# Eight-head attention on one Trainium2 core: the softmax is divided before the transposes on ScalarE instead of after the value product on VectorE, with a new order on every engine

## What is computed

```python
x = L0(x, ...)   # batch norm, 3x3 depthwise conv, 4-head attention on 7x7 keys, conv, 1x1, MLP
x = L1(x, ...)   # group norm, linear attention (softmax of k and of q apart), projection
# L2, the third layer
hid = group_norm(x, 32 groups)                      # (b, 256, 196)
q, k, v = split(einsum('oc,bcl->bol', qkv_w, hid) + qkv_b)      # 8 heads of 32 channels
weight = softmax(einsum('bhct,bhcs->bhts', q * scale, k * scale), axis=-1)
a = einsum('bhts,bhcs->bhct', weight, v)
x = x + einsum('oc,bcl->bol', proj_w, a) + proj_b
x = L3(x, ...)   # group norm, 1-head attention over 196 positions, projection, residual
```

## Time and profile before

| what | value |
|---|---|
| time, median of 3 runs | 2169.7 us (2168.6 to 2170.22) |
| the profiled execution's own time | 2170.37 us |
| its span, first to last instruction | 2168.3 us |
| mean granted TensorE clock | 0.976 |
| busy: PE, PEld | 2076.3 us (96%), 1686.7 us (78%) |
| busy: DVE, ACT, POOL | 1820.4 us (84%), 1527.8 us (70%), 1278.3 us (59%) |

### The profile page before, as it was taken

One profiled execution on the slowest core, in us unless ns is written; L12 is line 12 of the kernel. 1 busy time (PEld: TensorE's weight loads), 2 busy tenths in 40 slices (PEclk: granted clock), 3 DMA queues, 4 the chain that ended last, 5 costly groups with the idle time before them and its releaser, 6 DMA issues.

```text
span 2168.3 us, 58678 instructions
## 1 busy us (share of the span) xinstructions
PE 2076.3 (96%) x15232; PEld 1686.7 (78%) x15232; DVE 1820.4 (84%) x4359; ACT 1527.8 (70%) x5172; POOL 1278.3 (59%) x2954
## 2 busy tenths in 40 slices
PE   4679999999999999999999999999999999999987
PEld 3466888888888788888878888887888888788775
DVE  6778899988888998988899898888989888887532
ACT  2256777777777777777777777777777777777763
POOL 2455666666666666666666666666666666664311
PEclk8799999999999999999999999999999999999977
DMA  3000011001101100110110011011101100100000
GB/s 126 15 23 23 16 39 39 29 23 37 37 22 37 37 30 22 37 37 22 37 37 30 22 37 37 23 36 37 37 15 37 37 31 28 38 31 24 24 23 23
DMA packets 29828, 70.22 MB, mean 32 GB/s; under 512 B 6261, under 2 KB 7105, under 8 KB 29761
## 3 DMA queue, kind: packets, MB, share of 16 engines
q1 hardware_dynamic: 26928, 67.68, 9.0%
q10 hardware_dynamic: 2832, 1.73, 0.3%
HBM read 30.86 MB, written 12.85 MB: 20 GB/s over the span
## 4 chain that ended last, share of the span: by engine, by line
PE 91%; DVE 3%; POOL 2%; issue 2%; ACT 1%; SPq 1%; DMA 0%; POOLq 0%; DVEq 0%; ACTq 0%
PE ps_c L1166 19%; PE ps_a L1166 17%; PE ps_e L1166 17%; PE ps_b L1166 17%; PE ps_s L1166 10%; PE ps_s L1216 8%; POOL gn_t L579 1%; PE ps_a L1292 1%; DVE y L1158 1%; PE ps_e L1454 0%; PE ps_e L1292 0%; PE ps_b L1454 0%; PE ps_e L1399 0%; SPq L475 0%; ACT e L827 0%
## 5 line engine op out<-in xcount | busy, mean ns | idle before, releaser
L827 ACT ACTIVATE e<-ps_s,nm 98x196 f32<-98x196 f32 x1024 | 426.1, 446 | 89.9 <-DVE nm L956 89.8
L590 POOL TENSOR_SCALAR xn<-x,gn_scale,gn_shift 128x196 f32<-128x196 f32 x384 | 353.2, 933 | 20.8 <-POOL gn_shift L585 20.8
L1158 DVE SCALAR_TENSOR_TENSOR y<-opad,w_dw,y 128x406 f32<-128x406 f32 x512 | 301.8, 645 | 0.0
L1139 DVE SCALAR_TENSOR_TENSOR y<-xpad,w_dw,y 128x406 f32<-128x406 f32 x512 | 300.8, 640 | 0.0
L956 DVE TENSOR_REDUCE nm<-ps_s 98x4 f32<-98x784 f32 x256 | 240.6, 962 | 41.8 <-PE ps_s L1166 41.8
L834 ACT COPY pt<-ps_s 98x392 f32<-98x392 f32 x512 | 229.1, 503 | 42.6 <-PE ps_s L1216 41.8
L568 POOL TENSOR_TENSOR gn_t<-gn_group 128x4 f32<-128x4 f32 x96 | 34.3, 358 | 372.9 <-DVE gn_group L1006 286.5
L827 ACT ACTIVATION_READ_ACCUMULATOR e<-ps_s,nm 98x1 f32 x1024 | 231.6, 226 | 0.0
L1216 PE MATMUL ps_s<-w_eye,e 98*98 98x98 f32 x2048 | 204.6, 251 | 0.6 <-ACT e L827 0.6
L1216 PEld LDWEIGHTS ps_s<-w_eye,e 98*98 98x98 f32 x2048 | 186.3, 131 | 24.1 <-issue 16.2
L581 POOL TENSOR_SCALAR gn_t<-gn_t 128x4 f32<-128x4 f32 x288 | 119.7, 416 | 58.6 <-POOL gn_t L579 58.6
(11 more groups left out here) (245 smaller groups left out, 5596.8 us busy)
## 6 DMA issues: line engine op xcount, KB each, us to landing
x_in<-in_x SPq DMA_DIRECT2D x32, 392.0 KB, 3.1
x_res<-in_x SPq DMA_DIRECT2D x32, 392.0 KB, 3.3
x2b<-x SPq DMA_DIRECT2D x32, 392.0 KB, 2.6
out<-x SPq DMA_DIRECT2D x32, 392.0 KB, 2.6
out_pairs<-out SPq DMA_DIRECT2D x32, 392.0 KB, 3.5
w_q<-in_q SPq DMA_DIRECT2D x3, 256.0 KB
w_k<-in_k SPq DMA_DIRECT2D x3, 256.0 KB
w_v<-in_v SPq DMA_DIRECT2D x3, 256.0 KB
```

Source lines behind the costliest of these rows:

```text
L590: g.tensor_scalar(dst[:, c, of_image(i)], src[:, c, of_image(i)], t.scale[:, j:j + 1], t.shift[:, j:j + 1], ALU.mult, ALU.add).then_inc(t. ...
L827: s.activation(e2[:, j, tc], tile(use)[0:HALF, of_image(tc)], ACT.Exp, bias=nm2[:, j, tc:tc + 1], accum_out=den2[:, 2 * i + tc, h:h + 1]). ...
L1139: v.scalar_tensor_tensor(out=dst, in0=window(xpad, c, k, CR), scalar=tap, in1=dst, op0=ALU.mult, op1=ALU.add).then_inc(conv1_steps.sem, 1)
L1158: v.scalar_tensor_tensor(out=dst, in0=window(opad, c, k, CR), scalar=tap, in1=dst, op0=ALU.mult, op1=ALU.add).then_inc(conv2_steps.sem, 1)
```

## The change

1. `rden` is cut in eight: after each two heads of a group, DVE takes their reciprocals (98 x 4).
2. A new step `less{g}_{j}` on ACT multiplies the exponentials of a head, in place, by the reciprocal of their sum: two instructions of 98 x 196, SBUF to SBUF, 32 of them for a pair. `tn{g}_{j}` on PE now waits for them.
3. `rt` and `rep0`/`rep1` are gone on PE, ACT and DVE, and `an2`, `rt2` and `heads` with them; `proj` reads `a2`.
4. All five tables and the sharing of the banks are new. A pair's last step stands at slot 815 instead of 760, its first at 16 instead of 0.

```diff
-                        if p is not None:
-                            if g == 0:
-                                act.wait_ge(rden_done.sem, rden_done.at(p, 0))
...
+                            p = pair_of(t, u, ACT_AT[f"less{g}_{j}"])
+                            if p is not None:
+                                h = HG * (g % 2) + j
+                                act.wait_ge(rden_done.sem, rden_done.at(p, 2 * g + j // 2 + 1))
+                                for tc in range(2):
+                                    s.activation(e2[:, j, tc], e2[:, j, tc], ACT.Copy,
+                                                 scale=rden2[:, 2 * i + tc, h:h + 1]).then_inc(p2_done[j].sem, 1)
...
-                            if has_before(p):
-                                act.wait_ge(*read(p - 1, f"rep{g % 2}"))
+                            if has_before(p):
+                                act.wait_ge(*full(p - 1, latest("proj0", "proj1")))
...
-                        v.reciprocal(rden2[:], den2[:]).then_inc(rden_done.sem, 1)
+                                v.reciprocal(rden2[:, 2 * i:2 * i + 2, h:h + 2], den2[:, 2 * i:2 * i + 2, h:h + 2]
+                                             ).then_inc(rden_done.sem, 1)
-                        v.tensor_tensor(rt2[:, 1], tile("rt")[0:H2, 0:N2], rt2[:, 0], ALU.subtract).then_inc(emptied("rt"), 1)
-                            v.tensor_tensor(an2[:, :, c], tile(use)[:, 0:N2].rearrange("p (i n) -> p i n", i=2),
-                                            a2[:, :, c], ALU.mult).then_inc(emptied(use), 1)
...
-                                for source in elsewhere(use, f"sc{g}_{j}"):
-                                    pe.wait_ge(*read(p, source))
+                                pe.wait_ge(p2_done[j].sem, p2_done[j].at(p, 2 * g + 2))
...
-                        for j in range(4):
-                            last = nc.tensor.transpose(tile("rt")[0:H2, j * HALF:(j + 1) * HALF], rden2[:, j],
-                                                       eye[0:HALF, 0:HALF])
-                            product(tile(use)[:, 0:N2], lambda k: heads[:, c], lambda k: rt2[:, k]).then_inc(filled(use), 1)
-                            product(tile(use)[:, 0:N2], lambda k: w["p2"][:, k, of_chunk(c)], lambda k: an2[:, :, k]
+                            product(tile(use)[:, 0:N2], lambda k: w["p2"][:, k, of_chunk(c)], lambda k: a2[:, :, k]
...
-    "tn3_3": 498, "tn3_2": 499, "tn3_1": 501, "tn3_0": 503, "rt": 508, "av3": 515, "rep0": 537, "rep1": 539,
+    "tn3_3": 580, "tn3_2": 582, "tn3_0": 585, "av3": 611, "proj1": 623, "proj0": 625, "gn3": 643, "v3_1": 692,
```

More of the change, by code:

```diff
@@ L38 @@
 SP_AT = {
-    "x": -128, "res": 25, "hop": 358, "hop_out": 588, "store": 691,
+    "x": -77, "res": 256, "hop": 537, "hop_out": 742, "store": 844,
 }
 PE_AT = {
[9 rows of a table removed]
[9 rows of a table added]
 }
 ACT_AT = {
[11 rows of a table removed]
[13 rows of a table added]
 }
 DVE_AT = {
[10 rows of a table removed]
[11 rows of a table added]
 }
 POOL_AT = {
-    "resize0": 0, "resize1": 16, "probs0": 64, "probs1": 96, "gn1": 240, "gn2": 304, "gn3": 544, "rows3": 592,
+    "resize0": 96, "resize1": 112, "probs0": 160, "probs1": 176, "gn1": 336, "gn2": 400, "gn3": 640, "rows3": 704,
 }
 BANK_USES = {
[5 rows of a table removed]
+    "a": ("s0_1", "t0_1", "o0_0", "o0_1", "kv3", "ctx1", "out1", "gn2", "hk0", "hk1", "hq1", "proj0",
+          "v3_1", "v3_3", "t3_1",),
+    "b": ("s0_0", "v0", "kv1", "q1_1", "hv0", "gn3", "q3_0", "s3_1", "o3_1",),
+    "c": ("q0_1", "q0_0", "t0_0", "pw0", "mlp0", "kv2", "q1_0", "out0", "hq0", "proj1", "v3_2", "s3_0",
+          "o3_0",),
+    "e": ("k0", "pw1", "mlp1", "gn1", "kv0", "ctx0", "hv1", "q3_1", "v3_0", "t3_0",),
 }
@@ L236, in build @@
         a2 = sb("a2", [128, 2, KC, TOK])
-        an2 = sb("an2", [128, 2, KC, TOK])
         rden2 = sb("rden2", [HALF, 4, H2])
-        rt2 = sb("rt2", [H2, 2, N2], F32R)
         x3 = sb("x3", [128, KC, N2])
@@ L277, in build @@
         gn = {1: GroupNorm(1), 2: GroupNorm(2), 3: GroupNorm(3)}
-        PER_READ = {"k0": 2, "v0": 4, "rt": 1, "o0_0": 2, "o0_1": 2, "q1_0": 2, "q1_1": 2, "ctx0": 2, "ctx1": 2,
+        PER_READ = {"k0": 2, "v0": 4, "o0_0": 2, "o0_1": 2, "q1_0": 2, "q1_1": 2, "ctx0": 2, "ctx1": 2,
                     "s3_0": 2, "s3_1": 2, "o3_0": 2, "o3_1": 2}
@@ L358, in build @@
         max2_done = Count("max2_done", UNITS // 2)
-        rden_done = Count("rden_done", 1)
-        rt_high = Count("rt_high", 1)
+        rden_done = Count("rden_done", 2 * GROUPS)
+        p2_done = [Count(f"p2_done{j}", 2 * GROUPS) for j in range(HG)]
         l3_less_steps = Count("l3_less_steps", 2 * 3)
@@ L459, in build @@
         FOLDED = KC * 4
-        EARLY_STEPS = PLAIN + FOLDED + 7
+        EARLY_STEPS = PLAIN + FOLDED + 6
         @block.sync
@@ L660, in split_weights @@
                     s.copy(high, src).then_inc(early_high, 1)
-                s.copy(heads[:], w["heads"][:]).then_inc(early_steps, 1)
                 act.wait_ge(early_steps, EARLY_STEPS)
@@ L807, in step @@
                             s.copy(v2[:, i].rearrange("p c n -> p (c n)"), tile(use)[0:HALF, :]).then_inc(emptied(use), 1)
-                    p = pair_of(t, u, ACT_AT["rt"])
-                    if p is not None:
[L811 to L814, removed]
                     for g in range(GROUPS):
@@ L1051, in step @@
                                                    in1=xn1[:, c], op0=ALU.add, op1=ALU.add).then_inc(emptied(use), 1)
-                    p = pair_of(t, u, DVE_AT["rden"])
-                    if p is not None:
-                        for use in ends(*(f"sc{g}_{j}" for g in range(GROUPS) for j in range(HG))):
-                            dve.wait_ge(*read(p, use))
-                        if has_before(p):
-                            dve.wait_ge(*full(p - 1, "rt"))
-                        v.reciprocal(rden2[:], den2[:]).then_inc(rden_done.sem, 1)
-                    p = pair_of(t, u, DVE_AT["rt"])
-                    if p is not None:
-                        dve.wait_ge(rt_high.sem, rt_high.at(p, 1))
-                        v.tensor_tensor(rt2[:, 1], tile("rt")[0:H2, 0:N2], rt2[:, 0], ALU.subtract).then_inc(emptied("rt"), 1)
-                    for c in range(KC):
-                        use = f"rep{c}"
-                        p = pair_of(t, u, DVE_AT[use])
-                        if p is not None:
-                            dve.wait_ge(*full(p, use))
-                            if has_before(p) and not comes_after(use, latest("proj0", "proj1")):
-                                dve.wait_ge(*full(p - 1, latest("proj0", "proj1")))
-                            for source in ends(f"av{c}", f"av{2 + c}"):
-                                dve.wait_ge(*read(p, source))
-                            v.tensor_tensor(an2[:, :, c], tile(use)[:, 0:N2].rearrange("p (i n) -> p i n", i=2),
-                                            a2[:, :, c], ALU.mult).then_inc(emptied(use), 1)
+                    for g in range(GROUPS):
+                        i = g // 2
+                        for m in range(2):
+                            p = pair_of(t, u, DVE_AT[f"rden{g}_{m}"])
+                            if p is not None:
+                                for j in (2 * m, 2 * m + 1):
+                                    dve.wait_ge(*read(p, f"sc{g}_{j}"))
+                                h = HG * (g % 2) + 2 * m
+                                v.reciprocal(rden2[:, 2 * i:2 * i + 2, h:h + 2], den2[:, 2 * i:2 * i + 2, h:h + 2]
+                                             ).then_inc(rden_done.sem, 1)
                     for c in range(KC):
@@ L1392, in step @@
                                ).then_inc(filled(use), 1)
-                    p = pair_of(t, u, PE_AT["rt"])
-                    if p is not None:
-                        pe.wait_ge(*free(p, "rt"))
-                        pe.wait_ge(rden_done.sem, rden_done.at(p, 1))
-                        for j in range(4):
-                            last = nc.tensor.transpose(tile("rt")[0:H2, j * HALF:(j + 1) * HALF], rden2[:, j],
-                                                       eye[0:HALF, 0:HALF])
-                        last.then_inc(filled("rt"), 1)
-                    for c in range(KC):
-                        use = f"rep{c}"
-                        p = pair_of(t, u, PE_AT[use])
-                        if p is not None:
-                            pe.wait_ge(*free(p, use))
-                            for source in elsewhere(use, "rt"):
-                                pe.wait_ge(*read(p, source))
-                            product(tile(use)[:, 0:N2], lambda k: heads[:, c], lambda k: rt2[:, k]).then_inc(filled(use), 1)
                     for c in range(KC):
@@ L1414, in step @@
                             pe.wait_ge(*free(p, use))
-                            for source in elsewhere(use, "rep0", "rep1"):
```

(3 more changed lines are left out.)

6 lines of the change are left out of this document (2 added, 4 removed), and 66 rows, old and new, of tables (ACT_AT, BANK_USES, DVE_AT, PE_AT).

## The result

The changed kernel takes 2175.5 us (median of 11 runs, 2174.1 to 2181.2) where the kernel before, on the same chip, takes 2169.8 (11 runs): a ratio of 1.0031, 95% interval 1.0021 to 1.0040. It is slower by 0.3%. The forecast was 2152, faster; the time lies at the very top of its range, and its sign is wrong.

What follows compares the result with a forecast made beforehand. PE (TensorE), idle 0.25% in mid-run, was taken as the bound. Spans: 2168.3 - 33.9 (PE) + 8.7 (waits) + 3 (fill) + 5 (drain) = 2151.1 us; from the median 2169.7 - 17.2, said as 2152 us, range 2134 to 2176.

Steps and rivals of the forecast that it cites:

- the wait: PE waiting for ACT's copies in the loop, mainly at sc2: 0.3 us a round over 29 rounds, 8.7 us on.
- What PE loses: In each round, the removed rden transposes and rep0/rep1 free 1.17 us of PE; over 29 rounds 33.9 us off.
- The allowance of 0.2 us a round: On PE's reordered blocks, costed at nothing: 0.2 us a round to either side, 6 us in all.
- The meeting place: From sc1 to sc2: PE's work 15.78 us, ACT's 15.89, so the last copy ends 0.1 us late.
- The other three groups keep 1 us or more: At the attention groups other than sc1 to sc2, 1 us or more of air each, costed at nothing.
- What ACT gains: On ACT, less adds 12.1 us a round, making 58.8 of 61.89 us, 95%, still under the round.
- DVE: On DVE, seven more reciprocals against removed products: at or under 56.2 us a round, costed at nothing.
- Fill and drain: At the run's two ends: fill 3 us on (0 to 12.1), drain 5 on (4.5 off to 7.6 on).
- the chain of `rden`, `rt` and `rep`: In the last pair, from the last av copy to proj, this chain falls away: 4.5 us off.
- Nothing waits: Rival: no wait in the rounds, fill and drain cancel out, 2136 us; chance 0.10.
- ScalarE sets the pace: Rival at sc1 to sc2: ScalarE's waits decide from 0.89 us a round; 2187 us at 1.5; chance 0.15.
- TensorE wasn't the bound: Rival: the round stays at 63.06 us, held by something unnamed, only fill and drain change, 2178 us; chance 0.04.

Runs made afterwards that it cites:

- slot 0: The changed kernel with the first instruction of VectorE's loop body placed at slot 0 of a 256-instruction load block, nothing else changed: 2136.1 us, ratio 0.9839.
- 21 slots of shift: The changed kernel with 21 taken off each number of all five tables, and VectorE's loop head at slot 200: 2134.8 us, ratio 0.9838.
- The removed half alone, with its buffer: The kernel before without rt, rep0, rep1 and the product, with a plain copy of a2 into an2 in the product's place: 2134.5 us, ratio 0.9844.
- One copy more: The changed kernel with four more ScalarE copies a round, one per group, and the loop heads of VectorE and ScalarE at slot 0: 2164.0 us, ratio 0.9972.
- Without `less`: The changed kernel with VectorE's loop head at slot 0 and the 32 less steps deleted, attention left undivided: 2128.0 us, ratio 0.9805.
- the hint: The changed kernel with one instruction at the head of VectorE's loop body announcing the jump back, nothing placed: 2138.8 us, ratio 0.9853.
- slots 190 and 184: The changed kernel with VectorE's loop head placed at slot 190: 2224.8 us, ratio 1.0260; at slot 184: 2138.5 us, ratio 0.9850.

## Why the prediction was wrong

**The step that failed is the wait, "0.3 x 29 = 8.7 us on".** It was 1.7 us for each of the loop's 23 jumps, 40 us. Its cause is none that the prediction had: it counted work and waits of a round as if the round had no seam. The new table put a step on which ScalarE, and through it TensorE, waits directly behind the jump, and the new code put VectorE's body into a third block. Either alone would have been harmless: slot 0 takes away the second, 21 slots of shift the first, and each gives 39 to 41 us. The wait also stands at another place than forecast, at `ctx1` for `keys3`, not at `sc2` for the transposes' copies.

**What PE loses: right.** 1.17 us a round were forecast and a round went from 63.06 to 61.97 with slot 0, 1.09; over the 31 rounds between the pairs' first scores that is 30.2 us for the 33.9 forecast. The removed half alone, with its buffer, gave 27.2 there. The allowance of 0.2 us a round for the new order was ample.

**The meeting place: nearly right.** The sum said that ScalarE is 0.1 us short from `sc1` to `sc2`. With slot 0 nothing waits there: the last copy ends at 1031.28 us and `sc2` starts at 1031.42, 0.14 to spare. TensorE's own work there is 15.97 us (1015.45 to 1031.42), 0.2 more than the sum's 15.78, and covers what ScalarE was short. One copy more, 0.41 us of ScalarE, made the stretch 0.41 longer. So the forecast of 0.3 us was too high by 0.3, while the statement that this is the tightest place, and that no other has less, held. "The other three groups keep 1 us or more" did so only in part: with slot 0 the last copies end 0.69, 0.95 and 1.17 us ahead of `sc0`, `sc1` and `sc3`, and from `sc3` to `sc0` one copy more cost 0.3 of its 0.41, by a handover that no row singles out.

**What ACT gains.** The forecast was 58.8 us a round, 95%. With slot 0 it is 1671.73 / 1800 of a round of 61.97, 57.6 us, 93%. `less` is 1024 instructions, four in 1.53 us, so 0.38 each was right. **DVE**: 53.8 us a round, below the 56.2 of before, as said.

**Fill and drain: one right, one wrong in its sign.** The first scores come at 137.75 us with slot 0, where they came at 134.88: 2.9 on, forecast 3. From the last pair's `sc0` to the end it was 98.1 us and is 91.3: 6.8 off, forecast 5 on. Without `less` it is 89.0, so `less` costs about 2.4 us there and not 9.5. The removed half in the old order has 90.4, 7.7 off, where the prediction gave the chain of `rden`, `rt` and `rep` 4.5. But the granted clock over these last stretches isn't the same: 0.76 before, 0.83 with slot 0, 0.79 without `less`, 0.81 with the removed half. How much of each difference is the clock's and how much the work's stays open.

**The sum again, for the changed kernel:** spans 2168.3 + 1.0 (the first scores at 135.92) + 9.8 (the 31 rounds between: 1945.2 us for 1935.4) - 6.6 (the drain) = 2172.5, measured 2172.6. And with slot 0: 2168.3 + 2.9 - 30.2 - 6.8 = 2134.2, as measured.

**The rivals.** "Nothing waits", at 2136 us and 0.10, is the kernel with slot 0 to the microsecond. Its mechanism was right and underrated, the microsecond is luck: the rounds gave 3.7 us less than its 33.9, and fill and drain, which it let cancel out, gave 3.9 more. "ScalarE sets the pace" named the right size of wait to decide the sign, 0.89 us in a round, and was crossed, but by VectorE standing at the jump and not by ScalarE. "TensorE wasn't the bound" fell, and with it the rule of the Trainium skill, Perfetto Trace Analysis, section Identifying the Most-Contended Engine, as a forecast for this kernel: with weight loads busy for 81% the removed matmuls gave 1.09 of the 1.17 us a round that the idle time before matmuls had promised.

## What to carry to other kernels

A loop in a software pipeline has a seam: look at which step stands first behind the jump on each engine, and at how many instructions the body has there and where its head lies, before a timetable is compared with another. Otherwise a change of some instructions is measured together with a step in the time, here of 30 to 86 us, that has nothing to do with it; pin the head of the loop (or give the hint) in both kernels, then compare. And when an intermediate tile is removed, count it as a buffer too: what it decoupled will wait.

The best version is the change with VectorE's head at slot 0, 2136.1 us, 1.6% faster than the kernel before; the shift by 21 slots is as good.

## What the runs showed of the hardware

- A loop body of 325 instructions ran without a load when its head was at slot 0 or 184 of a block of 256, and loaded 5 packets of 8 KB for each jump at 190 and 200. From the jump to the body's first instruction it took 0.22 us in the first two and 3.37 and 2.72 in the others.
- VectorE stood 0.32, 1.8, 2.4 or 2.8 us at the jump. The 0.32 and the 1.8 belong to jumps of the same length (2.75 and 2.79 us), with 2.68 and 1.15 us of work in hand; the 2.4 to one of 2.91 with 0.63, the 2.8 to one of 3.37 with 0.80.
- Waits of TensorE of 1.1 to 1.5 us, one in each round, left its clock at 1.00 (the 2.4 GHz level). Of 23 waits of 2.1 to 2.5 us at the same place 10 were followed by a stretch at 0.50 (1.2 GHz). On the mean a round then lost 3.8 us (65.83 for 61.98 between slots 190 and 184) where TensorE's wait in it was 2.2.
- ScalarE showed the same: with 275 instructions in a round instead of 269 (44 of them reads of accumulators, which the profile shows as instructions of their own) the loads were back and its jump took 2.41 us, and with its head at slot 0 both were gone.
